# TensorE's order in each pair of row tiles of a 16-head attention, inside an adaptive-layernorm block with a routed FFN

## What is computed

```python
mod = (_silu(c) @ wmod).reshape(8, 6, 1, -1)          # sa, ca, ga, sb, cb, gb
h = _layernorm(x) * (1 + ca) + sa
# attention, 16 heads of 32: x is (8, 1024, 512)
q = (h @ Wq + bq).reshape(b, 16, 32, t)
k = (h @ Wk + bk).reshape(b, 16, 32, t)
v = (h @ Wv + bv).reshape(b, 16, 32, t)
attn = softmax(einsum('bhdt,bhds->bhts', k, v) * temperature, axis=-1)
x = x + ga * einsum('bhdt,bhts->bhds', q, attn).reshape(b, t, d)
h = _layernorm(x) * (1 + cb) + sb
# of each batch the 512 tokens with the highest score h . w_router go through
# a gelu FFN (512 -> 2048 -> 512) and are added back times sigmoid(score) * gb
```

## Time and profile before

| | |
|---|---|
| median of 3 runs | 2256.76 us (2256.72 to 2259.34) |
| the profiled execution, its own time | 2256.3 us |
| its span | 2254.6 us |
| start of group 1 to end of group 30's last piece | 98.53 to 1524.74 us |
| group 31 | 1524.74 to 1572.29 us |
| busy: TensorE matmuls, VectorE, ScalarE, GpSimd | 98%, 83%, 63%, 62% |
| chain that ended last, by engine | PE 56%, DVE 32%, POOL 5% |

### The profile page before, as it was taken

The page is one execution under the profiler, slowest core; times in us unless marked ns, Lnnn a source line. Parts: engine busy times, 40 slices in busy tenths (PEclk is TensorE's granted clock), DMA queues, the critical chain, the costliest instruction groups (busy, mean ns, idle before and its releaser), DMA issues.

```text
span 2254.6 us, 35231 instructions
## 1 busy us (share of the span) xinstructions
PE 2204.0 (98%) x12410; PEld 841.5 (37%) x12410; DVE 1876.2 (83%) x2885; ACT 1425.7 (63%) x2478; POOL 1407.8 (62%) x1178
## 2 busy tenths in 40 slices
PE   6999999999999999999999999997999999999998
PEld 3333333333333333333333333331444444444443
DVE  6999999999999999999999999999884563563533
ACT  3788888888888888888888888888321111111110
POOL 6878887777887788877888787874552302312300
PEclk9999999999999999999999999999999999999999
DMA  8443355353345434434533543443332112212200
GB/s 258 98 101 87 88 114 108 85 116 88 84 100 114 89 92 109 92 94 106 100 86 92 125 83 93 96 83 115 110 102 71 61 48 71 73 36 71 70 29 19
DMA packets 218864, 206.06 MB, mean 91 GB/s; under 512 B 139256, under 2 KB 139288, under 8 KB 218176
## 3 DMA queue, kind: packets, MB, share of 16 engines
q1 hardware_dynamic: 208176, 174.12, 33.9%
q0 software_dynamic: 9728, 25.23, 3.7%
q10 hardware_dynamic: 784, 4.47, 0.6%
HBM read 71.37 MB, written 43.19 MB: 51 GB/s over the span
## 4 chain that ended last, share of the span: by engine, by line
PE 56%; DVE 32%; POOL 5%; issue 3%; ACT 3%; DMA 0%; ACTq 0%; SPq 0%; POOLq 0%; DVEq 0%
DVE nmax L1149 22%; PE sc L854 13%; PE sc L841 13%; PE acc L700 10%; PE sc L651 10%; PE pj L675 7%; POOL x L1537 3%; PE pj L663 3%; ACT probs L922 2%; DVE qn L1201 2%; DVE stats L1183 2%; DVE dot_out L1169 1%; DVE x L1178 1%; DVE rinv L1196 1%; POOL hbuf L1546 0%
## 5 line engine op out<-in xcount | busy, mean ns | idle before, releaser
L922 ACT ACTIVATE probs<-sc,nmax 128x1024 f32<-128x1024 f32 x1024 | 1137.8, 1116 | 232.9 <-DVE nmax L1149 223.6
L1149 DVE TENSOR_REDUCE nmax<-sc 128x1 f32<-128x1024 f32 x1024 | 1206.1, 1214 | 31.6 <-PE sc L651 28.3
L700 PE MATMUL acc<-probs,qn 128*32 128x512 f32 x4096 | 545.8, 605 | 5.0 <-DVE x L1178 2.6
L1025 ACT ACTIVATE probs<-sc,b_col 128x512 f32<-128x512 f32 x128 | 87.9, 687 | 523.8 <-PE sc L841 481.5
L663 PE MATMUL pj<-room 128*128 128x512 f16 x1500 | 385.5, 379 | 3.8 <-POOL room L1490 2.9
L854 PE MATMUL sc<-room,probs 128*128 128x512 f16 x1536 | 352.1, 379 | 0.7 <-DVE room L1229 0.7
L651 PE MATMUL sc<-stacks 128*128 128x512 f16 x1024 | 308.2, 383 | 10.7 <-ACT probs L922 9.1
L651 PE MATMUL sc<-room 128*128 128x512 f16 x1024 | 307.9, 382 | 7.0 <-ACT probs L922 3.4
L1367 DVE CAST probs<-probs 128x512 f16<-128x512 f32 x128 | 62.2, 486 | 276.1 <-ACT probs L1025 230.8
L854 PEld LDWEIGHTS sc<-room,probs 128*128 128x128 f16 x1536 | 150.2, 98 | 182.2 <-DVE room L1229 1.2
L663 PEld LDWEIGHTS pj<-room 128*128 128x128 f16 x1500 | 143.7, 98 | 187.6 <-ACT room L893 12.1
(11 more groups left out here) (170 smaller groups left out, 2311.6 us busy)
## 6 DMA issues: line engine op xcount, KB each, us to landing
stacks<-room SPq DMA_DIRECT2D x512, 64.0 KB, 2.0
room<-room SPq DMA_DIRECT2D x508, 64.0 KB, 2.0
h_rows<-hbuf SPq DMA_DIRECT2D x132, 128.0 KB
out<-base SPq DMA_DIRECT2D x132, 128.0 KB
room<-in_L_attn_x SPq DMA_DIRECT2D x96, 128.0 KB, 2.8
rows<-mod_rows SPq DMA_DIRECT2D x32, 256.0 KB, 4.7
room<-in_L_ffn_W SPq DMA_DIRECT2D x8, 1024.0 KB, 5.1
f_lo<-first_rows SPq DMA_DIRECT2D x16, 256.0 KB, 3.9
```

Of the source, the lines that this page charges most:

```text
L700: mm = nc.tensor.matmul(acc[at:at + DH, :], qn[:, (p // 2) % 2, p % 2, h2, :], probs[:, (2 * p + h2) % PROBS, half * D:(half + 1) * D], st ...
L922: nc.scalar.activation(probs[:, u % PROBS, :], slot(b, g, ring_at(p, h2)), ACT.Exp, bias=nmax[:, u % PROBS:u % PROBS + 1], accum_out=rsum[ ...
L1025: nc.scalar.activation(g32[:, f % 2, :], ff[f % 2], ACT.Gelu_apprx_tanh, bias=b1_col[:, f:f + 1], scale=1.0 / WS).then_inc(gelu_done, 1)
L1149: nc.vector.tensor_reduce(nmax[:, u % PROBS:u % PROBS + 1], slot(b, g, ring_at(p, h2)), AX.X, ALU.max, negate=True).then_inc(max_done, 1)
```

## The change

In `body`, the call for the pair's first scores moves from ahead of the products to behind them, and that for the second scores from ahead of the piece to behind it. The wait for a group's `stacks` at pairs 0 and 8 stays at the top of the pair.

```diff
                             for k in range(2):
                                 pe.wait_ge(s_stk[k][g % 2][p // NQ], stk_count(b, g))
 
-                        scores_of(b, g, p, 0)
                         if b == 0 and g == 0 and p < LAG:
...
                             products((p - LAG) % PAIRS).then_inc(pv_done, 1)
-                        scores_of(b, g, p, 1)
+                        scores_of(b, g, p, 0)
                         if end:
                             if p in KEPT_AT:
...
                         else:
                             whole(piece)
+                        scores_of(b, g, p, 1)
```

## The result

The change makes the kernel slower by 6.8%: 2410.75 us, the median of four runs (2406.59 to 2412.28), against 2257.2; the ratio is 1.0677 with a 95% interval of 1.0663 to 1.069. Forecast were 2404 us, between 2350 and 2460. The profiled execution took 2410.43 us; its span is 2408.7, 154.1 more than before.

The account below looks back on a forecast made before the run. The prediction held that TensorE paces each group without a gap, so new waits add: 5.26 us a group less today's 0.53, times 30, is 142; with opening and last group 148, giving 2404 us, range 2350 to 2460.

Parts of the forecast that it names:

- "not slower" rival: VectorE is the pacemaker and TensorE's steps hide latency that stalls could fill: 2256 us, chance 0.04 (with no effect).
- piece, pair 3: TensorE's piece waits for ScalarE's evacuation in pair 2, behind that pair's first exponentials: 0.78 us a group.
- products, pair 4: TensorE's products wait for the gated copy behind pair 3's first maximum: 0.99 us, 0.78 already paid, so 0.21 more.
- piece, pair 6: TensorE's piece waits for ScalarE's evacuation behind pair 5's first exponentials: 0.57 us a group.
- piece, pair 9: TensorE's piece waits for ScalarE's evacuation of values behind pair 8's first exponentials: 1.01 us a group.
- products, pair 12: TensorE's products wait for the gated copy behind pair 11's first maximum: 0.80 us, hiding the piece's own 0.48.
- piece, pair 14: TensorE's piece waits for ScalarE's evacuation of queries behind pair 13's first exponentials: 0.93 us a group.
- piece, pair 0: TensorE's piece waits for ScalarE's evacuation of queries behind pair 15's first exponentials: 0.96 us a group.
- x: VectorE's other work directly ahead of a pair's first maximum: 0.68 us at pair 2, 0.47 at 5 and 11, 1.00 at 8.
- The lag formula: Time from a pair's first scores to VectorE's maximum: 0.29 us plus VectorE's other work directly ahead, at least 0.64.
- the rivals with shrunken or persisting lags: Delays from scores to maximum shrink further, 2318 to 2370 us, chance 0.12; or stay, 2440 to 2468, chance 0.06.
- The rival: TensorE's clock falls in each group because of its new idles: 2463 us, chance 0.06.

Follow-up runs that it names:

- experiment 1: Changed kernel with ScalarE's six evacuations of a group moved ahead of the pair's first exponentials: 2320.64 us.
- Experiment 6: Changed kernel with one VectorE statistics instruction done twice in pair 7, ahead of pair 8's first maximum, the copy's result unused: 2427.11 us.
- experiment 9: Changed kernel with two GpSimd steps swapped in each group, the third slice's split (ending in L1479) ahead of the first row product L1546: 2402.62 us.
- Experiment 5: Kernel before with only the first scores moved, behind the products: 2315.69 us.
- experiments 2 to 9: The eight follow-up runs after the first, each an edit of the scores' order, other steps' places or VectorE's work: from 2263.93 to 2427.11 us.

## Why the prediction was right

**The pacemaker.** TensorE had no gap to fill, so each new wait was added to the time. The "not slower" rival falls with experiments 1 and 6: what TensorE waits for moves the time one for one (experiment 1: 3.0 us of waits less and 2.9 us of time less in a group).

**The places and sizes of the waits**, a group:

| wait at | forecast | measured |
|---|---|---|
| piece, pair 3 | 0.78 | 0.75 |
| products, pair 4 | 0.21 | 0.22 |
| piece, pair 6 | 0.57 | 0.48 |
| piece, pair 9 | 1.01 | 0.96 |
| products, pair 12 | 0.80 | 1.26 |
| piece, pair 14 | 0.93 | 0.65 |
| piece, pair 0 | 0.96 | 1.05 |
| together | 5.26 | 5.37 |

The sum is as near as it is because errors cancel; that part is luck. At pair 12 the x of 0.47 for `q_over_sums` was too small: the quotients there run under GpSimd's L1479, x is 0.81 and the lag 1.13, not 0.76 (experiment 9). The step of 0.05 from the end of a wait to TensorE's start was read at one evacuation; it is 0.06 at pairs 3, 6, 9 and 14, but 0.15 behind the gated copy and at pair 0. That is 0.10 more at pairs 12 and 0; at pair 4 it is offset by a lag of pair 3 of 0.85, not 0.95. At pair 14 the lag is 1.13, not 1.41: x is below the 1.12 of the forecast, since the quotients take 0.29 there and one of the three rank counts, L104, 0.34 us on average in place of the 1.33 of the kernel before, where it too ran beside L1479. So the row of one rank count was fair, but x at both pairs depended on where GpSimd stood, which the forecast did not look at.

**The lag formula.** 0.29 + x gave 0.97, 1.29 and 1.44 for pairs 2, 8 and 15; the trace has 0.93, 1.25 and 1.43. At pairs 5, 11 and 13 it gave 0.76, 0.76 and 1.41, and the trace has 0.66, 1.13 and 1.13: there x itself was off (0.38, 0.81 and 0.85 were measured), and with the measured x the formula holds within 0.03. Backlog did vanish and work directly ahead did stay, as argued; the rivals with shrunken or persisting lags had those of pairs 2, 8 and 15 at 0.64 or at 1.2 to 1.95, as in the kernel before. Experiment 6 added 0.6 to one lag and got it back in the time. Experiment 5 shows how far the formula is only as good as the steps in it.

**The net.** 142 us were forecast for groups 1 to 30, 146.5 measured; 4 for the opening, 3.2 measured; 2 for the last group, 1.2 measured. The opening is near for another reason than the one given: the forecast put its 4 us in group 0 from pair 4 on, where 1.2 were lost; the other 2.0 were lost before pair 4. Nothing was forecast for the rest, which takes 3.3 more. Around the start of the FFN the granted clock is 0.86 over 12 us (1723 to 1735) in the changed kernel and 1.00 at the same place before (1572 to 1584), and the FFN's first batch takes 82.0 us against 80.3. Experiment 1 has both, 0.86 and 81.9; in experiments 2 to 9 the first batch takes 80.3 to 80.4. That is some 1.7 of the 3.3. Of the rest, 1.0 lies between the last scores and the FFN's first matmul and 0.6 in the FFN's second batch; what brings them about stays open, and so does what brings the clock down there. In the opening the first scores now stand behind pair 0's share of the modulation, for whose weights TensorE waits 5.66 us of DMA: they start at 45.28 us, not at 40.23; by pair 1 all but 1.0 of these 5 us is made up.

**The clock.** 1.00 in groups 1 to 30, with 5.4 us of waits a group; 0.96 in the last group, as before. The rival fell: waits of up to 1.7 us between groups of matmuls did not make the clock swing here. Among the experiments, with waits like these, one fall stands in groups 1 to 30: in experiment 1 the clock is 0.50 for 3.3 us, from 534.2. The rule of the Trainium skill that was set beside the sum ("TensorE: Matmul & The Clock Gate", section "A second HAM failure mode: psum-queue depth-cycling") would have had it swing; the measured 1.00 decides.

## What to carry to other kernels

Before moving work on a full engine, ask for each wait in its stream what chain leads to it, where the chain starts, and how much of that engine's own work lies between the start and the wait; the loss is the chain less that work, and a slack of half a microsecond is spent at once when a step of 1.5 moves. A chain often runs through another engine's program order: here an evacuation stood behind an exponential it has nothing to do with. If an order has to change, move those along with it, both of them: the evacuations alone gave back 90 of the 154 us, the gated copy alone nothing, both 142. One alone can uncover a wait that the other had hidden, or lengthen its chain.

## What the runs showed of the hardware

VectorE's quotients L1201 (float32, two inputs in SBUF) take 0.29 us alone. Begun while GpSimd runs L1479 or, in experiment 9, L1546 (each with two inputs in SBUF), they end 0.14 to 0.15 us after it, in each of 31 cases under L1479 in either kernel and in each of 31 under L1546. In experiment 9, 0.24 us less for one such copy a group was worth 7 us of the kernel's time, where a chain led through it. The maxima L1149, which read PSUM, take 1217 ns on average in the changed kernel and 1214 before, and none takes over 1.23 us, so they show no such thing. The Trainium skill, "SBUF — State Buffer", section "SBUF: two separate sides", says that a VectorE instruction with two SBUF inputs and a GpSimd one that reads SBUF take a shared pair of ports as a whole, and the later one waits for the earlier to finish; the 0.15 us here agree with it.
